# A post-norm decoder layer on one core: the end of the cross attention and the start of the experts rewritten

## The chip, the cores and the metric

The kernel runs on one core of one Trainium2 chip. Its engines work side by side and meet through semaphores: PE (TensorE, matrix products and transposes, results in PSUM), DVE (VectorE), ACT (ScalarE), POOL (GpSimd), and SP (SyncE), which here only issues DMAs. The metric is the device time of one execution in microseconds (us), as the median of several; lower is better. TensorE's clock has two levels, 1.2 and 2.4 GHz; the profile gives the granted clock as a share of the upper one.

## What is computed

One decoder layer for B = 8 batches of T = 512 tokens of D = 256 values, in float32 at the interface:

```python
x = layernorm(x + self_attention(x))            # 16 heads, decayed, levelled weights
x = layernorm(x + cross_attention(x, ctx))      # 16 heads, 1024 context tokens
x = layernorm(x + ffn(x))
# ffn, 32 experts:
probs  = softmax(x @ gate_w.T + gate_b, axis=tokens)     # per expert, over the 512 tokens
vals, idx = top_k(probs, 8)                              # each expert picks 8 tokens
merged = sum over the 8 of x[idx] * vals                 # [B, E, D]: one vector per expert
h = gelu([merged, 1] @ w1[e]);  o = [h, 1] @ w2[e]       # w1: 257x1024, w2: 1025x256
out[idx] += o * vals
```

## The kernel before, in words

There are three stages, each a block with one instruction stream per engine, and a barrier between blocks: `self_attention` (to about 620 us), `cross_attention` (to about 1717 us), `experts_and_combine` (the rest).

**Cross attention.** The work of a batch is cut into 32 steps `s`. In each step PE makes two pairs of score products (L1352, released to ACT for the exponential L1485), four products whose row maxima DVE takes (L1284, read by DVE at L1583, for the maxima 12 steps ahead), and four products of weights and values of the step before (`values`, L1306: four 32-column outputs in four column groups of the array). ACT evacuates one lane of PSUM (`cpsA`, 2 slots), DVE another (`cpsV`, 3 slots); a slot is taken in the order of a fixed job list, so PE can start a job of DVE's lane only when DVE has read the job three places before it. What closes the **previous** batch is spread over the steps of the current one, at fixed steps: MERGE (4) transposes the attention output, PROJECT_O (5) multiplies by Wo for four groups of 128 tokens, and DVE adds the residual and takes the layer norm's statistics (`stats`, `mv`); POOL makes `rstd`; NORM (7) applies it to `o2`; X2T (9) transposes `o2` for the gate; COPY_X2 (10); GATE (13) makes the gate's logits `L` and, on DVE, the 8 largest (`m8`), their negated maximum (`nm8`) and `L2`, a copy of `L` with those 8 replaced by -3e38; GATE_EXP (15): ACT takes exp of `L` and of `L2`; TOP8 (16): the difference of the two, divided by the sum, is `P8`, which is zero but for the 8 picked tokens; TOP8_T (17) transposes it; PICK (28) multiplies it with the tokens, which gives `mg` = merged; PICK_T (29) transposes `mg` into `sh.mT`. In the first batch there is no previous one; batches 1 to 7 carry this work, batches 1 to 6 in a loop on all engines but PE. After batch 7 the same steps run once more, alone: the **tail** (section `tail`, 30 steps with nothing but them).

The end of `cross_attention` on SP: in batch 7 it already loads the weights of the first two groups of experts (`w1_0`, `w2_0`, `w1_1`, `w2_1`), each group 4 experts, 4 MB of w1 and 4 MB of w2.

**Experts.** The 32 experts run in 8 groups `n`, with two buffers for w1 and two for w2. For a group PE makes the first product (L1840, 16 matmuls of 128x512, `mg4` times `w1`), transposes the result (L1850), DVE adds the bias, ACT applies gelu, PE makes the second product (L1864). SP loads ahead: `w1` of group n+2 may go when group n's first product is done (`h_full`), `w2` of group n+2 when its second product is done (`o_full`). In front of that, SP issues 14 small loads at the block's start: `b1r` (bias rows), `pick`, four times `b2` and eight times `p8`. PE at its start waits for `b1r` and transposes it (L1826), then waits for `pick` and `b2` (`c_loaded`) and for POOL's zeroed tiles (`zeroed`), and only then begins group 0. POOL at its start zeroes `hT`, `mg4[0]` and `mg4[1]` (L1775) and then copies `sh.mT` into them (L1780).

```python
            for n in range(2, GROUPS):
                sp.wait_ge(h_full, n - 1)
                load_group_weights(sp, sh, dram, 1, n % 2, n * EG)
                sp.wait_ge(o_full, n - 1)
                if n < GROUPS - 1:
                    load_group_weights(sp, sh, dram, 2, n % 2, n * EG)
```

## Time and profile before

| | |
|---|---|
| time, median of 3 runs | 1894.79 us (1892.1 to 1896.41) |
| profiled execution, its own time | 1894.31 us |
| profiled execution, span in the trace | 1892.4 us |
| busy: PE / DVE / ACT / POOL | 1698.3 / 1232.2 / 848.5 / 595.6 us |
| granted TensorE clock, mean | 0.954 |
| cross attention | about 620 to 1717 us |
| experts and combine | about 1717 to 1892 us |

The span is what the trace covers; the time is some 2 us longer. A row of a timeline gives the start, the duration, the engine, the line, the operation with output and input, how many instructions were merged into it, and in square brackets how long the engine had been idle before and what ended that. "x8" behind a float32 matmul counts passes: a float32 matmul is two of them.

### The profile page before, as it was taken

The numbers are of one execution on the slowest core, as the hardware profiler recorded it, in microseconds if no ns is written. First come the engines' busy times: TensorE is split into PE (matmuls) and PEld (weight loads), VectorE is DVE, ScalarE is ACT, GpSimd is POOL, SyncE is SP. The second block draws the span as 40 slices with busy tenths as digits, with TensorE's granted clock in tenths as the row PEclk, the third lists the DMA queues.
The fourth block names the chain that finished last, engine by engine and source line by source line (L and its number), as shares of the span: only waits on it lengthen the run. The fifth ranks groups of instructions, "written<-read, shape, count | busy, mean of one in ns | idle before, by whom it ended". The sixth has DMA issues, their size and how long they took to land. (4 is left out here: it accounts for less than half of the span.)

```text
span 1892.4 us, 48907 instructions
## 1 busy us (share of the span) xinstructions
PE 1698.3 (90%) x19908; PEld 811.1 (43%) x19908; DVE 1232.2 (65%) x2427; ACT 848.5 (45%) x1029; POOL 595.6 (31%) x955
## 2 busy tenths in 40 slices
PE   5999999999995599999999999999999999976654
PEld 3566666666664233343333333433433334232222
DVE  5767667766753577867778778678677788811004
ACT  3324334334332126655556556566555565651103
POOL 3535555555532715033043140250430410000002
PEclk8999999999997679999999999999999999988887
DMA  7000000000000321111202101111112023245994
GB/s 245 3 3 3 3 3 3 3 3 3 3 3 2 98 73 39 43 44 53 74 1 68 59 26 52 49 51 40 37 53 74 1 76 117 91 178 192 421 419 147
DMA packets 60477, 135.15 MB, mean 71 GB/s; under 512 B 11088, under 2 KB 34128, under 8 KB 52592
## 3 DMA queue, kind: packets, MB, share of 16 engines
q1 hardware_dynamic: 60272, 132.18, 19.3%
q8 instruction: 157, 2.57, 0.6%
q14 instruction: 48, 0.39, 0.1%
HBM read 89.29 MB, written 4.72 MB: 50 GB/s over the span
## 5 line engine op out<-in xcount | busy, mean ns | idle before, releaser
L1583 DVE TENSOR_REDUCE mx<-cpsV 128x1 f32<-128x512 f32 x1024 | 652.7, 685 | 196.4 <-PE cpsV L1284 182.4
L1485 ACT ACTIVATE w<-cpsA 128x1024 f32<-128x1024 f32 x512 | 496.6, 1023 | 291.1 <-PE cpsA L1352 284.5
L1284 PE MATMUL cpsV<-w 96*128 96x512 bf16 x1024 | 329.1, 393 | 34.9 <-DVE mx L1583 23.4
L1352 PE MATMUL cpsA<-w 99*128 99x512 bf16 x1024 | 273.2, 380 | 11.4 <-ACT w L1457 5.9
L1306 PE MATMUL cacc<-w 128*32 128x512 f32 x2048 | 281.1, 604 | 0.4 <-ACT w L1485 0.4
L1139 POOL TENSOR_TENSOR w<-w,zero 128x256 bf16<-128x256 f32 x84 | 48.8, 612 | 579.9 <-ACTq L1458 579.9
L1284 PEld LDWEIGHTS cpsV<-w 96*128 96x128 bf16 x1024 | 85.6, 98 | 304.9 <-DVE mx L1583 203.9
L606 ACT COPY QK<-psA 128x1024 f32<-128x1024 f32 x64 | 64.8, 1013 | 228.2 <-PE psA L363 228.2
L1352 PEld LDWEIGHTS cpsA<-w 99*128 99x128 bf16 x1024 | 92.5, 97 | 148.5 <-ACT w L1457 16.2
L714 POOL TENSOR_TENSOR VP<-V,VPF 128x128 f32<-128x128 f32 (+2 forms) x256 | 128.5, 532 | 41.4 <-PE psA L376 36.1
L363 PE MATMUL psA<-XT,wq 128*128 128x512 f32 x256 | 130.7, 634 | 4.7 <-issue 2.9
L363 PE MATMUL psA<-XT,wk 128*128 128x512 f32 x256 | 126.9, 618 | 1.3 <-DVE WT L921 1.3
L930 DVE TENSOR_TENSOR tmp<-psV,CF 128x512 f32<-128x512 f32 x64 | 44.3, 692 | 119.3 <-PE psV L426 119.0
L1914 DVE TENSOR_TENSOR z<-psE,b1T 128x256 f32<-128x256 f32 x8 | 3.4, 425 | 127.9 <-PE psE L1850 127.9
L1306 PEld LDWEIGHTS cacc<-w 128*32 128x32 f32 x2048 | 43.3, 108 | 92.8 <-issue 76.0
L937 DVE TENSOR_REDUCE Y<-tmp 128x128 f32<-128x512 f32 x64 | 67.7, 1058 | 5.1 <-issue 0.5
L1840 PE MATMUL psE<-w,mg 128*32 128x512 f32 x256 | 40.7, 794 | 29.6 <-DMA w<-in_w 26.1
L1457 ACT COPY w<-cpsA 128x1024 f32<-128x1024 f32 x24 | 24.3, 1012 | 95.7 <-PE cpsA L1254 49.7
L1271 PEld LDWEIGHTS cpsA<-w,w 128*128 128x128 f32 x512 | 58.4, 192 | 14.3 <-ACT w L1485 12.6
L1555 POOL TENSOR_TENSOR crstd<-cmv,eps 128x4 f32<-128x4 f32 x8 | 1.6, 202 | 199.4 <-DVE cmv L105 199.4
L396 PEld LDWEIGHTS psV<-QK 64*32 64x32 f32 x4096 | 41.3, 106 | 49.7 <-issue 48.4
L363 PEld LDWEIGHTS psA<-XT,wq 128*128 128x128 f32 x256 | 44.4, 193 | 41.8 <-issue 37.2
(219 smaller groups left out, 2350.1 us busy)
## 6 DMA issues: line engine op xcount, KB each, us to landing
w<-in_w SPq DMA_DIRECT2D x60, 1024.0 KB, 22.4
w<-w SPq DMA_DIRECT2D x192, 128.0 KB, 2.3
w<-w SPq DMA_DIRECT2D x192, 64.0 KB, 2.0
w<-in_ctxT SPq DMA_DIRECT2D x8, 1024.0 KB, 5.2
XT<-in_xT SPq DMA_DIRECT2D x8, 512.0 KB, 6.1
x_tok<-in_x SPq DMA_DIRECT2D x8, 512.0 KB, 10.1
w<-in_w SPq DMA_DIRECT2D x8, 512.0 KB, 21.3
out_y<-w SPq DMA_DIRECT2D x16, 256.0 KB, 2.4
```

The lines of the kernel that those rows point to most:

```text
L363: last = nc.tensor.matmul(out[:, n * T:(n + 1) * T], w[:, k, i * P:(i + 1) * P], XT[:, b, k, :], start=(k == 0), stop=(k == KD - 1))
L606: nc.scalar.copy(QK[:, i % 4, :], full(("qk", i))).then_inc(act_evac, 1)
L714: last = nc.gpsimd.tensor_tensor(VP[:, p % 2, g, 0:n, :].rearrange("q n (h c) -> q n h c", c=HD), vv.unsqueeze(1).broadcast_to([P, n, 2, HD]),
L930: nc.vector.tensor_tensor(tmp[:].rearrange("p g s (h c) -> p (g s) h c", c=HD), src.rearrange("p (h x) -> p h x", h=2)[:, :, 0:4 * HD * G] ...
L937: nc.vector.tensor_reduce(yp, tmp[:].rearrange("p g s c -> p g c s"), AX_X, ALU.add)
L1139: ops.tensor_tensor(cut(high, c), cut(r, c), zeros, ALU.add)
L1271: last = nc.tensor.matmul(out[:, c * P:(c + 1) * P], cT[:, k, c * P:(c + 1) * P], wv[:, k, hv * P:(hv + 1) * P], start=(k == 0), stop=(k = ...
L1284: nc.tensor.matmul(out, Qst[q // 2][0:ROWS, hh, g * P:(g + 1) * P], Kst[q // 2][0:ROWS, hh, half * BANK:(half + 1) * BANK], start=True, st ...
L1306: last = nc.tensor.matmul(acc[BLK * jj:BLK * (jj + 1), :], Vc[:, c, 4 * q + jj, :], Pr[:, (2 * s + jj // 2) % 4, (jj % 2) * T:(jj % 2 + 1) ...
L1352: last = nc.tensor.matmul(out[:, n * T:(n + 1) * T], Kst[q // 2][0:ROWS + 3, hh, c * P:(c + 1) * P], Qst[q // 2][0:ROWS + 3, hh, :], start ...
L1485: nc.scalar.activation(Pr[:, (2 * s + pp) % 4, :], src, ACT.Exp, scale=CA_SCALE).then_inc(act_evac, 1)
L1583: nc.vector.tensor_reduce(mx[:, q % 2, row, k % 2:k % 2 + 1], full(m[k]), AX_X, ALU.max).then_inc(dve_evac, 1)
```

## The change

Six edits. **(a)** PICK: the four products of the token groups, which were added up in one 32-row output, go to four 32-row outputs in four column groups of the array; `mg` now holds four partial sums one above the other, and PICK_T adds them up while transposing, by a product with `sum4` (four identity matrices of 32 in a column) in place of two transposes. `mg` is evacuated on 128 partitions, split by `k`. **(b)** One exponential: ACT takes exp of `L` alone, into `EL`, as soon as `nm8` is there (DVE's `match_replace` goes on meanwhile), and TOP8 keeps those elements of `EL` whose `L2` is below -1e38. **(c)** NORM counts `x2_ready` up once per token group, with no drain, and X2T waits group by group. **(d)** In PROJECT_O the statistics of groups 0 and 1 are taken between the additions of groups 1 and 2. **(e)** Experts, PE: group 0's first product goes to the front; the transposes of `b1r` and the wait for `pick` and `b2` follow it; the wait for `zeroed` is ACT's alone. **(f)** Experts, POOL: `mg4[0]` is zeroed and filled first, then `mg4[1]`, then `hT` is zeroed. DVE makes `sum4` once at the start of the cross attention.

```diff
@@ PE, cross attention
                         if s == PICK:
                             out = take_v("mg", after="p8T")
                             for g in range(G):
-                                last = nc.tensor.matmul(out[0:E, 0:D], P8T[:, g, :], o2[:, g, :],
-                                                        start=(g == 0), stop=(g == G - 1))
+                                last = nc.tensor.matmul(out[E * g:E * (g + 1), 0:D], P8T[:, g, :], o2[:, g, :],
+                                                        start=True, stop=True)
...
                             for k in range(KD):
-                                last = nc.tensor.transpose(out[:, k * P:(k + 1) * P],
-                                                           mgp[:].rearrange("e (p k) -> e k p", k=KD)[:, k, :], sh.ident[:])
+                                last = nc.tensor.matmul(out[:, k * P:k * P + E], mgp[:, k, :], sum4[:],
+                                                        start=True, stop=True)
...
                     if prev and s == X2T:
-                        pe.wait_ge(x2_ready, b)
-                        transpose_x("x2T", o2)
+                        out = take_a("x2T")
+                        for g in range(G):
+                            pe.wait_ge(x2_ready, (b - 1) * G + g + 1)
+                            for k in range(KD):
+                                last = nc.tensor.transpose(out[:, k * T + g * P:k * T + (g + 1) * P],
+                                                           o2[:, g, k * P:(k + 1) * P], sh.ident[:])
+                        last.then_inc(act_full, 1)
@@ ACT, cross attention
                         if s == GATE_EXP:
                             act.wait_ge(l_ready, b)
-                            nc.scalar.activation(L[:], L[:], ACT.Exp, bias=nm8[:, 0:1], accum_out=sume[:, 0:1])
-                            nc.scalar.activation(L2[:], L2[:], ACT.Exp, bias=nm8[:, 0:1])
+                            nc.scalar.activation(EL[:], L[:], ACT.Exp, bias=nm8[:, 0:1], accum_out=sume[:, 0:1])
                             act.drain().then_inc(e_ready, 1)
@@ DVE, cross attention
+            nc.vector.tensor_reduce(sum4[:], sh.ident[:].rearrange("p (g e) -> p e g", e=E), AX_X, ALU.add)
...
                             for g in range(G):
                                 nc.vector.tensor_tensor(o2[:, g, :], full(("wo", g))[:, 0:D], xb(b - 1)[:, g, :], ALU.add
                                                         ).then_inc(dve_evac, 1)
+                                if g % 2:
+                                    dve.drain()
+                                    for gg in (g - 1, g):
+                                        nc.vector.bn_stats(stats[:, gg, :], o2[:, gg, :])
                             dve.drain()
-                            layer_norm_stats(nc, dve, o2, stats, mv).then_inc(var, 1)
+                            for g in range(G):
+                                last = nc.vector.bn_aggr(mv[:, g, :], stats[:, g, :])
+                            last.then_inc(var, 1)
...
                                 nc.vector.tensor_scalar(o2[:, g, :], o2[:, g, :], mv[:, g, 0:1], rstd[:, g, 0:1],
-                                                        ALU.subtract, ALU.mult)
-                            dve.drain().then_inc(x2_ready, 1)
+                                                        ALU.subtract, ALU.mult).then_inc(x2_ready, 1)
...
-                            nc.vector.tensor_scalar(nm8[:], m8[:, 0:1], -1.0, None, ALU.mult)
+                            nc.vector.tensor_scalar(nm8[:], m8[:, 0:1], -1.0, None, ALU.mult).then_inc(l_ready, 1)
                             nc.vector.match_replace(L2[:], m8[:], L[:], -3.0e38)
-                            dve.drain().then_inc(l_ready, 1)
+                            dve.drain()
...
-                            nc.vector.tensor_tensor(P8, L[:], L2[:], ALU.subtract)
+                            nc.vector.scalar_tensor_tensor(out=P8, in0=L2[:], scalar=-1.0e38, in1=EL[:],
+                                                           op0=ALU.is_lt, op1=ALU.mult)
...
-                            nc.vector.tensor_copy(mg, full("mg")[0:E, 0:D]).then_inc(dve_evac, 1)
+                            nc.vector.tensor_copy(mgp[:], full("mg")[:, 0:D].rearrange("q (p k) -> q k p", k=KD)
+                                                  ).then_inc(dve_evac, 1)
@@ PE, experts
-            pe.wait_ge(b_loaded, 16)
-            for c in range(FC):
-                last = nc.tensor.transpose(psB[:, c * E:(c + 1) * E],
-                                           b1r[:].rearrange("e (p c) -> e c p", c=FC)[:, c, :], sh.ident[0:E, 0:E])
-            last.then_inc(b1_full, 1)
-            pe.wait_ge(c_loaded, 16 * (1 + BT))
-            pe.wait_ge(zeroed, 1)
             for n in range(GROUPS):
...
                 last.then_inc(h_full, 1)
-                if n:
+                if n == 0:
+                    pe.wait_ge(b_loaded, 16)
+                    for c in range(FC):
+                        last = nc.tensor.transpose(psB[:, c * E:(c + 1) * E],
+                                                   b1r[:].rearrange("e (p c) -> e c p", c=FC)[:, c, :], sh.ident[0:E, 0:E])
+                    last.then_inc(b1_full, 1)
+                    pe.wait_ge(c_loaded, 16 * (1 + BT))
+                else:
                     pick_rows(n - 1)
```

**PE at the start of the experts.** The stream of PE from the last step of the tail on; `psE` is the PSUM of the experts, `mg_0` is `mg4[0]`, `w_0` a weight buffer, `sum` is `sum4`. Before:

```order
L1388 MATMUL cpsV<-o,P8T 32x256 x4
L1394 MATMUL cpsV<-ident,mg 128x128 x2
L1068 UNCONDITIONAL_BRANCH
L1793 UNCONDITIONAL_BRANCH
L1826 MATMUL psE<-ident,b1r 128x32 x8
L1840 MATMUL psE<-w_0,mg_0 32x512 x16
L1850 MATMUL psE<-ident,hS 128x128 x8
```

And in the changed kernel:

```order
L1388 MATMUL cpsV<-o,P8T 32x256 x4
L1394 MATMUL cpsV<-sum,mg 128x32 x2
L1068 UNCONDITIONAL_BRANCH
L1807 UNCONDITIONAL_BRANCH
L1847 MATMUL psE<-w_0,mg_0 32x512 x16
L1854 MATMUL psE<-ident,b1r 128x32 x8
L1864 MATMUL psE<-ident,hS 128x128 x8
```

The first product (16 matmuls) has moved ahead of the 8 transposes of `b1r`; the two transposes of `mg` have become two products of 32 columns.

**POOL at the start of the experts.** The memsets and the copies that release PE's first product, of before and of the change:

```order
-L1775 MEMSET hT 128x1024
-L1775 MEMSET mg_0 128x256
-L1775 MEMSET mg_1 128x256
-L1780 COPY mg_0<-mT 128x8x8
-L1780 COPY mg_1<-mT 128x8x8
```

```order
+L1788 MEMSET mg_0 128x256
+L1794 COPY mg_0<-mT 128x8x8
+L1788 MEMSET mg_1 128x256
+L1794 COPY mg_1<-mT 128x8x8
+L1791 MEMSET hT 128x1024
```

One memset and one copy stand before `mg_0` is ready, where there were three memsets and one copy.

**DVE at PROJECT_O and after, in the tail.** Additions of the residual (`o<-cpsV,x_tok`), statistics (`BN_STATS`), their aggregate, the norm and the gate. Before:

```order
L1640 TENSOR_TENSOR o<-cpsV,x_tok 128x256 x4
L102 BN_STATS cstats<-o 128x6 x4
L105 BN_AGGR cmv<-cstats 128x2 x4
L1647 TENSOR_SCALAR o<-o,cmv,crstd 128x256 x4
L1651 TENSOR_SCALAR L<-cpsV,gb 32x512
```

And in the changed kernel:

```order
L1645 TENSOR_TENSOR o<-cpsV,x_tok 128x256 x2
L1650 BN_STATS cstats<-o 128x6 x2
L1645 TENSOR_TENSOR o<-cpsV,x_tok 128x256 x2
L1650 BN_STATS cstats<-o 128x6 x2
L1653 BN_AGGR cmv<-cstats 128x2 x4
L1658 TENSOR_SCALAR o<-o,cmv,crstd 128x256 x4
L1661 TENSOR_SCALAR L<-cpsV,gb 32x512
```

Two of the four statistics have moved between the additions; nothing else changes its place on this engine, in the tail or in the batches.

## Rows read from the trace of the kernel before

**Rows 1.** Busy time by stretch: PE, PEld, DVE, ACT, POOL, then clock, DMA share, GB/s

```profile
760.00:1500.00 740.00, 709.90 (x3890) 276.95 (x3883) 561.01 (x1136) 422.38 (x457) 199.27 (x320) 1.00 0.14 46
1683.00:1717.00 34.00, 18.39 (x52) 10.26 (x50) 10.15 (x32) 4.39 (x6) 1.31 (x3) 0.70 0.54 225
1755.00:1805.00 50.00, 28.75 (x300) 12.86 (x296) 0.85 (x2) 3.97 (x7) 0.47 (x2) 0.85 1.01 420
```

**Rows 2.** Timeline at the start of the experts

```profile
1716.90 0.96 POOL L1775 MEMSET hT<- 128x1024 f32 x1 [20.15 <-POOLq L1068]
...
1718.53 0.41 POOL L1780 COPY mg<-mT 128x64 f32<-128x64 f32 x2 [0.17 <-issue]
...
1719.15 1.09 PE L1826 MATMUL psE<-ident,b1r 32*128 32x32 f32 x8 [2.85 <-DMA b1r<-in_w]
...
1722.38 0.89 SPq L1754 DMA_DIRECT2D p<-p_scratch  x2
...
1723.81 6.04 PE L1840 MATMUL psE<-w,mg 128*32 128x512 f32 x32 [3.57 <-DMA b<-in_w]
...
1729.92 2.00 SPq L998 DMA_DIRECT2D w<-in_w  x4
```

**Rows 3.** Timeline, the first products of groups 3 and 7

```profile
1763.60 4.93 PE L1840 MATMUL psE<-w,mg 128*32 128x512 f32 x32 [6.07 <-DMA w<-in_w]
...
1843.14 6.11 PE L1840 MATMUL psE<-w,mg 128*32 128x512 f32 x32 [6.21 <-DMA w<-in_w]
```

**Rows 4.** Timeline of the tail: last addition, statistics, norm, transposes

```profile
1692.95 0.42 DVE L1640 TENSOR_TENSOR o<-cpsV,x_tok 128x256 f32<-128x256 f32 x1 [0.44 <-PE cpsV L1368]
1693.47 1.40 DVE L102 BATCH_NORM_STATS2 cstats<-o 128x6 f32<-128x256 f32 x4
...
1696.78 1.38 DVE L1647 TENSOR_SCALAR o<-o,cmv,crstd 128x256 f32<-128x256 f32 x4 [1.46 <-POOL crstd L1557]
...
1698.25 1.97 PE L1246 MATMUL cpsA<-ident,o 128*128 128x128 f32 x8 [5.34 <-DVEq L1649]
```

**Rows 5.** Timeline of the tail: replacing the eight, exponentials, reciprocal

```profile
1706.74 0.66 DVE L1657 MATCH_REPLACE8 L<-m,L 32x512 f32<-32x512 f32 x1
1707.46 0.72 ACT L1499 ACTIVATE L<-L,nm 32x512 f32<-32x512 f32 x1 [5.25 <-DVEq L1658]
...
1708.18 0.70 ACT L1500 ACTIVATE L<-L,nm 32x512 f32<-32x512 f32 x1
1708.94 0.15 DVE L1663 RECIPROCAL rsum<-sume 32x1 f32<-32x1 f32 x1 [1.54 <-ACTq L1501]
```

**Rows 6.** Timeline of the tail: pick, its copy, its transposes

```profile
1711.79 3.50 PE L1388 MATMUL cpsV<-o,P8T 128*32 128x256 f32 x8 [0.38 <-DVE P8T L1668]
...
1715.33 0.41 DVE L1671 COPY mg<-cpsV 32x256 f32<-32x256 f32 x1 [3.60 <-PE cpsV L1388]
1715.80 0.51 PE L1394 MATMUL cpsV<-ident,mg 128*128 128x128 f32 x2 [0.51 <-DVE mg L1671]
```

**Rows 7.** Timeline inside a batch, around its PICK step

```profile
1174.20 1.06 PE L1306 MATMUL cacc<-w 128*32 128x512 f32 x8
...
1177.03 1.70 PE L1388 MATMUL cpsV<-o,P8T 128*32 128x256 f32 x7
...
1177.96 1.29 DVE L1583 TENSOR_REDUCE mx<-cpsV 128x1 f32<-128x512 f32 x2
...
1179.17 0.40 DVE L1671 COPY mg<-cpsV 32x256 f32<-32x256 f32 x1
...
1180.17 1.29 DVE L1583 TENSOR_REDUCE mx<-cpsV 128x1 f32<-128x512 f32 x2 [0.59 <-PE cpsV L1284]
```

**Rows 8.** Timeline inside a batch, PE after its PROJECT_O step

```profile
1094.32 0.39 PE L1284 MATMUL cpsV<-w 96*128 96x512 bf16 x1 [0.54 <-DVE mx L1583]
```

**Rows 9.** Timeline of batch 7, ACT after the PICK step

```profile
1674.54 1.94 ACT L1485 ACTIVATE w<-cpsA 128x1024 f32<-128x1024 f32 x2 [1.74 <-PE cpsA L1352]
```

**Rows 10.** Timeline, nearest passes with full weights and few columns

```profile
763.66 3.84 PE L1271 MATMUL cpsA<-w,w 128*128 128x128 f32 x32
```

More of the change, by code:

```diff
@@ L1097, in cross_attention @@
         stats, mv, rstd = sb("cstats", [P, G, 6]), sb("cmv", [P, G, 2]), sb("crstd", [P, G, 1])
-        L, L2 = sb("L", [E, T]), sb("L2", [E, T])
-        P8p, mgp = sb("P8", [P, T]), sb("mg", [P, D])
-        P8, mg = P8p[0:E], mgp[0:E]
+        L, L2, EL = sb("L", [E, T]), sb("L2", [E, T]), sb("EL", [E, T])
+        P8p, mgp = sb("P8", [P, T]), sb("mg", [P, KD, P])
+        P8, sum4 = P8p[0:E], sb("sum4", [P, E])
         m8, nm8, sume, rsum = sb("m8", [E, 8]), sb("nm8", [E, 1]), sb("sume", [E, 1]), sb("rsum", [E, 1])
@@ L1494, in body @@
                         if s == COPY_X2:
-                            act.wait_ge(x2_ready, b)
+                            act.wait_ge(x2_ready, b * G)
                             nc.scalar.copy(xb(b - 1), o2[:]).then_inc(x2_copied, 1)
@@ L1521, in _ @@
         def _(pool):
-            for t in (Vc, NM, P8p, mgp):
+            for t in (Vc, NM, P8p):
                 nc.gpsimd.memset(t[:], 0.0)
@@ L1773, in _ @@
         def _(pool):
-            for t in (hT, mg4[0], mg4[1]):
-                last = nc.gpsimd.memset(t[:], 0.0)
-            pool.drain().then_inc(zeroed, 1)
             for n in range(GROUPS):
+                if n < 2:
+                    nc.gpsimd.memset(mg4[n][:], 0.0)
+                    pool.drain()
+                if n == 2:
+                    nc.gpsimd.memset(hT[:], 0.0).then_inc(zeroed, 1)
                 if n >= 2:
```

## The prediction

> **What bounds the kernel now.** I read the busy time by stretch first. In the batches of the cross attention PE is busy 709.9 of 740 us with the clock at its upper level, so PE sets the pace there and DVE, at 561, has little slack. In the tail (1683 to 1717) PE is busy 18.4 of 34 us at a granted clock of 0.70 and every other engine less: nothing is full, a chain of dependent steps is the bound. From 1755 on the DMA engines are at 1.01 with 420 GB/s: the stream of expert weights is the bound [rows 1]. That stream of 48 MB (six groups of w1 and w2) cannot start before group 0's first product is done: the timeline has the product at 1723.81, 6.04 us long, and the first weight load right behind it at 1729.92 [rows 2]. So what makes the first product end earlier starts the stream earlier, and with it all that follows. Three places then count for the sum: the seven closings inside the batches, the tail, and the start of the experts.
>
> **Start of the experts (e, f).** Before, PE stood idle for `b1r`, transposed it (1.09 us), then waited for `b2` until 1723.81. Now it needs only `mg4[0]` and weights that were loaded long before. POOL begins at 1716.90; zeroing 1024 columns took 0.96 us, so 256 take at most 0.3; one copy is half of 0.41 [rows 2]. With 0.15 us for a drain and hand-over that makes 1717.55 for the start of the product, 6.26 earlier than 1723.81. If the product keeps its 6.04 us, it ends at 1723.6. What is late next is SP: its 14 small loads end at 1722.38 + 0.89 = 1723.27 [rows 2], so the load could not go before 1723.3 anyway. Gain 6.25. The product's duration depends on the clock: later ones took 4.93 and 6.11 us [rows 3], and wholly at 1.2 GHz it would be about 7.0 (8 passes of `values` take 1.06 at the upper level, some 0.2 of it the pipeline's end [rows 7]; 32 passes are 3.4, doubled 6.8, plus 0.2). So the gain lies between 5.3 (7.0 us product) and 6.6 (SP's queue). The moved transposes of `b1r` (1.09) now lie beside ACT's evacuation of the product and cost at most 0.1; memset of `hT` is done before ACT needs it. The cover for these is the weight stream, which has 4 MB under way by then; without it they would cost their 1.1 us.
>
> **Tail.** Each term is on the chain, so it counts in full. (d) Two of four statistics (half of 1.40) fall into PE's time for groups 2 and 3, where DVE idled 0.44 before the addition [rows 4]: -0.70. (c) The transposes started at 1698.25, behind all four normalizations; the first group is ready after a quarter of 1.38, at 1697.13, and two transposes (0.49) take longer than one normalization (0.35), so PE runs through from 1697.2: -1.04 [rows 4]. (b) ACT can start when `match_replace` starts (1706.74), 0.66 earlier, and the second exponential's 0.70 goes, of which I leave 0.1 for the read of the first one's accumulator, which it hides now. So the reciprocal comes at 1707.7 in place of 1708.94: -1.26. `match_replace` ends at 1707.40, just in time [rows 5]. The comparison and product that replaces the subtraction has the same two inputs and size and is taken as equal. (a) The pick took 3.50 us, 8 passes one behind the other at the lower clock level [rows 6]. In four column groups they run side by side: `values` has that form, four outputs of 32 rows, 8 passes of twice the columns, in 1.06 at the upper level [rows 7], so about 0.43 for the passes there, 0.86 at the lower level, 1.1 with the end: -2.4. The copy `mg` reads as many elements per partition: 0.41. PICK_T has four passes in place of two, with full weights and few columns. Two took 0.51 [rows 6]; four cost 1.02 at that pace, or 0.5 by the pace of 3.84 us for 32 [rows 10], which is the upper level: +0.45, bounds 0 and +0.5. Sum of the tail: -0.70 - 1.04 - 1.26 - 2.4 + 0.45 = -4.95.
>
> The Trainium skill, in "TensorE: Matmul & The Clock Gate", section "LDWEIGHTS (loading the stationary operand)", speaks against (a) here: a weight load takes time by its columns, about 107 ns for 128, so shrinking the moving side to 32 columns saves little. By it four loads would be 0.43 us and the term near 0; the row at the lower level asks for more.
>
> **Inside the batches.** (a) Around the PICK step in a batch the passes take 1.7 us one after the other (eight times 0.21) and would take 0.43: PE is freed 1.28. But DVE is next. After the pick it still has two maxima, 1177.96 to 1179.25, then the copy of `mg` to 1179.57, and only at 1180.17 the next maximum, after an idle 0.59 [rows 7]. With PE earlier DVE goes on at 1179.6, and PE waits for its slots: so 0.6 of the 1.28 arrives. In batch 7, which has no maxima at step 28, ACT stood idle 1.74 before it [rows 9] and PE's 1.28 arrives nearly whole: 1.15. (d) After PROJECT_O, PE waits 0.54 for DVE, which is behind by its 1.4 us of statistics [rows 8]; the same row is there in batches 1 to 6, 0.53 to 0.54. With 0.7 us of statistics moved into DVE's idle gaps of 0.44 between additions, that wait goes and PE's next issues move up: 0.6, bounds 0.5 and 0.7. (b) The exponential dropped lies on ACT, which has room; DVE is full at the TOP8 step, so nothing arrives. (c) needs nothing here: X2T is two steps behind NORM. PICK_T's two more passes cost PE two times 0.12 [rows 10], half of it behind other waits: +0.1. Per batch 0.6 + 0.6 - 0.1 = 1.1, times six is 6.6; batch 7 gives 1.15 + 0.6 - 0.1 = 1.65. Together -8.2. Bounds: 0, if all of it is swallowed by DVE; 7 x (1.28 + 0.7) = 13.9, if all arrives. `sum4` and one memset fewer lie at the block's start under PE's first products: 0.
>
> **Sum.** -8.2 - 4.95 - 6.25 = -19.4. Against the profiled execution's own 1894.31 that is 1874.9; the median of the runs is 0.5 higher, so 1875.
>
> **Rivals.**
> *DVE swallows the batches' part.* The closing work in the batches then brings 0 and only tail and start count: -11.2, 1883. For it: DVE has waits of its own to give and the maxima follow back to back at these places. Against it: the idle 0.59 and PE's wait of 0.54 are in the trace and must close. Chance 0.15. The Trainium skill, in "TensorEngine Tiling (Array Packing)", section "PSUM Bottleneck", says this: tiling speeds up the array but not the reading of PSUM, which may become the bound after it. The trace agrees for half of the gain.
> *PE's time counts in full.* PE is at 96% in the batches, and after a few steps DVE could have caught up: -13.9 - 4.95 - 6.25 = -25.1, 1869.5. Against it: the slots of `cpsV`. Chance 0.12.
> *The early product starts nothing.* If SP or the stream itself is later than I think (the small loads and w1 share the DMA engines; or the end hangs on PE's last group rather than on the stream), the 6.25 is lost: -13.15, 1881.5. Against it: in rows 1 the DMA engines are full. Chance 0.07.
> *No change.* The stages hide it all, within 3.8 us. I see no cover for the tail's chain: 0.03.
> *Slower.* PE's clock falls inside the batches. Every us of PE work at 1.2 GHz costs another us. Place: the steps where column groups now run side by side and leave PE short gaps waiting for DVE. 2.8 us of such work in each of seven batches eats the 19.4, and from there it is slower; 5 us per batch would cost 35 and give 1894.8 - 19.4 + 35 = 1910. Against it: the granted clock is 1.00 over 740 us although PE waits 0.5 to 1 us at several places per batch [rows 1, 8]. Chance 0.03.
>
> **How the numbers follow.** The likeliest case, 0.60, is 1875, own range 1872 to 1878 (batches 5.5 to 11, start 5.3 to 6.6). The range 1869 to 1883.5 reaches to the cases on both sides. Changes within 0.2% (3.8 us) can't be told from none here. Faster 0.94, same 0.03, slower 0.03.
>
> **What would show it.** First product at about 1.0 us after the block's start, before `b1r`'s transposes, and the first w1 load at its end, some 6.7 us after the block's start in place of 13.0; the stretch from there to the end unchanged at 162.5. In the tail the pick near 1.1 us, its transposing near 1.0, the reciprocal 0.95 after `match_replace` begins. In the batches a period shorter by 1.1 us, DVE's idle 0.59 gone and PE's 0.54 gone. Wrong it would be most easily in the batches: if the period moves by 0 or by 2, the interplay of DVE and PE was misread; and if the product takes 7 us, the start is worth a microsecond less.

## The result, and the profile after

| | before | after |
|---|---|---|
| time, median | 1895.15 us (1892.1 to 1896.41, 4 runs) | 1879.16 us (1874.29 to 1881.4, 4 runs) |
| profiled execution: its time, span | 1894.31, 1892.4 us | 1881.4, 1879.5 us |
| granted TensorE clock, mean | 0.954 | 0.949 |

The ratio is 0.9912, interval 0.9895 to 0.9929: 16.7 us less, where the sum had 19.4. The forecast's 1875 lies 4.2 us below the new median and the range holds it. One execution of all, 2007.93 us at a mean clock of 0.821 (in "More work for PE instead"), was in a slow state of the chip and is left out. Two numbers ask for a closer look: the profiled execution gained only 12.9 us of span (it was the slowest of its four), and the mean clock went down. So the three places of the sum are read one by one. The stretches between the same marks in both traces:

| stretch, us | before | after | difference | forecast |
|---|---|---|---|---|
| block's start to first exponential of the batches | 684.35 | 684.58 | +0.2 | 0 |
| first to last exponential of the batches | 995.28 | 993.86 | -1.4 | -8.2 |
| last exponential to the end of `mT` (tail) | 36.98 | 32.33 | -4.65 | -4.95 |
| end of `mT` to the first w1 load | 13.31 | 6.71 | -6.6 | -6.25 |
| first w1 load to the end | 162.46 | 162.06 | -0.4 | 0 |

Tail and start came as computed; in the batches 6.8 us are missing. The busy time by stretch of the changed kernel, columns as in [rows 1]:

```profile
760.00:1500.00 740.00, 710.50 (x3903) 277.37 (x3902) 563.28 (x1136) 419.68 (x450) 198.00 (x318) 0.99 0.14 46
1683.00:1717.00 34.00, 21.49 (x86) 11.19 (x86) 9.39 (x27) 3.78 (x5) 3.13 (x7) 0.60 0.59 234
...
1755.00:1805.00 50.00, 31.70 (x344) 14.55 (x336) 1.27 (x3) 5.26 (x9) 0.71 (x3) 0.86 1.01 421
```

The first row answers to [rows 1]: PE is busy about as long, but the clock there reads 0.99 in place of 1.00. That hundredth of 740 us is the riddle of this case.

**Start of the experts**, the timeline that answers to [rows 2]:

```profile
1711.04 0.32 POOL L1788 MEMSET mg<- 128x256 f32 x1 [16.12 <-POOLq L1068]
...
1711.49 0.24 POOL L1794 COPY mg<-mT 128x64 f32<-128x64 f32 x1
...
1711.87 5.05 PE L1847 MATMUL psE<-w,mg 128*32 128x512 f32 x32 [1.42 <-POOL mg L1794]
...
1716.54 0.89 SPq L1766 DMA_DIRECT2D p<-p_scratch  x2
...
1716.85 1.06 PE L1854 MATMUL psE<-ident,b1r 32*128 32x32 f32 x8
...
1717.47 2.10 SPq L998 DMA_DIRECT2D w<-in_w  x4
```

The product begins 0.83 us after POOL does and is done at 1716.92; the load goes only at 1717.47, behind SP's last small load (1716.54 + 0.89 = 1717.43). The bound of 6.6 that the prediction gave for a faster product is what came: SP's queue is late next.

**Tail**, the rows that answer to [rows 4 to 6]:

```profile
1691.77 0.42 DVE L1645 TENSOR_TENSOR o<-cpsV,x_tok 128x256 f32<-128x256 f32 x1 [0.56 <-PE cpsV L1368]
1692.29 0.75 DVE L1650 BATCH_NORM_STATS2 cstats<-o 128x6 f32<-128x256 f32 x2
...
1694.96 1.39 DVE L1658 TENSOR_SCALAR o<-o,cmv,crstd 128x256 f32<-128x256 f32 x4 [1.47 <-POOL crstd L1561]
...
1695.52 1.94 PE L1415 MATMUL cpsA<-ident,o 128*128 128x128 f32 x8 [3.78 <-DVE o L1658]
...
1704.01 0.66 DVE L1667 MATCH_REPLACE8 L<-m,L 32x512 f32<-32x512 f32 x1
1704.05 0.72 ACT L1504 ACTIVATE EL<-L,nm 32x512 f32<-32x512 f32 x1 [4.60 <-DVE nm L1666]
...
1704.91 0.15 DVE L1673 RECIPROCAL rsum<-sume 32x1 f32<-32x1 f32 x1 [0.24 <-ACTq L1505]
...
1707.76 1.08 PE L1388 MATMUL cpsV<-o,P8T 128*32 128x256 f32 x8 [0.38 <-DVE P8T L1679]
...
1708.91 0.42 DVE L1682 COPY mg<-cpsV 128x256 f32<-128x256 f32 x1 [1.20 <-PE cpsV L1388]
...
1709.39 1.06 PE L1394 MATMUL cpsV<-sum,mg 128*128 128x32 f32 x4 [0.55 <-DVE mg L1682]
```

Statistics behind the last addition: 1.40 to 0.75. Start of the normalization to start of the transposes: 1.47 to 0.56. Start of `match_replace` to the reciprocal: 2.20 to 0.90. Pick: 3.50 to 1.08. Its transposing: 0.51 to 1.06.

One thing in this stretch was luck. The product with Wo at its start is the same in all kernels, but its time hangs on the granted clock. In the traces of before, of the change, and of a second execution of the change (experiment "The changed kernel once more"):

```profile
1687.32 5.59 PE L1368 MATMUL cpsV<-cwo,oT 128*128 128x256 f32 x16 [1.10 <-ACT oT L1447]
```

```profile
1685.26 6.47 PE L1368 MATMUL cpsV<-cwo,oT 128*128 128x256 f32 x16 [1.10 <-ACT oT L1452]
```

```profile
1684.67 3.72 PE L1368 MATMUL cpsV<-cwo,oT 128*128 128x256 f32 x16 [1.10 <-ACT oT L1452]
```

With the transposes in front of it, which took 1.95, 1.09 and 1.09, it comes to 7.54, 7.56 and 4.81. The first two happen to be equal, so the difference of the two stretches shows the edits alone. In the second execution of the change the stretch took 29.57 in place of 32.33, and these products account for all of the 2.8.

**Inside a batch.** Answers to [rows 8] (the first row) and [rows 7] (the rest):

```profile
1094.40 0.65 PE L1284 MATMUL cpsV<-w 96*128 96x512 bf16 x2
...
1178.97 0.64 PE L1388 MATMUL cpsV<-o,P8T 128*32 128x256 f32 x8
...
1179.91 1.29 DVE L1588 TENSOR_REDUCE mx<-cpsV 128x1 f32<-128x512 f32 x2
1181.11 0.42 DVE L1682 COPY mg<-cpsV 128x256 f32<-128x256 f32 x1
1181.44 1.28 DVE L1588 TENSOR_REDUCE mx<-cpsV 128x1 f32<-128x512 f32 x2
```

PE's wait of 0.54 is gone, the pick's passes take 0.64 in place of 1.7, and the idle 0.59 of DVE behind the copy is gone too. These signs of the forecast all came. To see why the gain didn't arrive, take the time of every step: the distance between every second exponential of ACT. For batch 2, all steps that differ by 0.1 us or more, worked out from the exponentials' starts:

```
step                6     15     16     17     28     29
before           3.54   3.47   2.29   5.54   4.60   3.40
after            2.89   2.86   2.81   5.69   4.15   3.30
difference      -0.65  -0.61  +0.52  +0.15  -0.45  -0.10
```

The sum is -1.14, and -1.1 was forecast. Batch 6 gained 1.35 and batch 7 2.0. If all had gone so, the batches would have gained some 9 us. But in batches 1, 3, 4 and 5 step 17 took 7.08 to 7.27, and step 5 of batch 0, where no closing exists, was longer as well. The timeline at step 17 of batch 3, changed kernel (PE, then DVE):

```profile
1138.21 0.38 PE L1284 MATMUL cpsV<-w 96*128 96x512 bf16 x1
1139.74 0.39 PE L1284 MATMUL cpsV<-w 96*128 96x512 bf16 x1 [1.15 <-DVE mx L1588]
1140.34 0.66 PE L1325 MATMUL cpsV<-ident,OT 128*128 128x128 f32 x4 [0.21 <-DVE mx L1588]
1141.03 0.83 PE L1382 MATMUL cpsV<-ident,P 128*128 128x128 f32 x4
1141.79 1.94 PE L1306 MATMUL cacc<-w 128*32 128x512 f32 x8
1143.66 1.03 PE L1284 MATMUL cpsV<-w 96*128 96x512 bf16 x2
...
1137.07 1.15 DVE L1674 SCALAR_TENSOR_TENSOR P<-L,EL 32x512 f32<-32x512 f32 x1
1138.30 0.79 DVE L1677 TENSOR_SCALAR P<-P,rsum 32x512 f32<-32x512 f32 x1
```

and the same place before the change:

```profile
1139.39 0.39 PE L1284 MATMUL cpsV<-w 96*128 96x512 bf16 x1 [1.01 <-DVE mx L1583]
...
1140.67 0.63 PE L1382 MATMUL cpsV<-ident,P 128*128 128x128 f32 x4
1141.23 1.06 PE L1306 MATMUL cacc<-w 128*32 128x512 f32 x8
```

The same eight passes of `values` take 1.94 in place of 1.06. Busy time by stretch, 3 us of it and then the whole time at the lower level, changed kernel:

```profile
1141.00:1144.00 3.00, 2.97 (x13) 0.79 (x14) 1.55 (x7) 0.00 (x0) 0.00 (x0) 0.55 0.43 135
1141.30:1144.70 3.40, 3.40 (x15) 0.80 (x14) 1.65 (x8) 0.00 (x0) 0.00 (x0) 0.50 0.38 118
```

The granted clock is 0.50 for 3.4 us: PE ran at 1.2 GHz there, busy without a pause, soon after the wait of 1.15 (0.7 to 1.6 us after it ended, in the four batches). Each such fall cost 1.4 to 1.6 us. The profile of before has none in the batches, that of after has five: some 7.5 us, which covers the 6.8 that are missing.

Batch 6 had no fall, and it had no long wait either. There POOL, which is a pass ahead and in batches 1 to 5 adds `bo` to a later batch's tokens beside DVE's two operations (first row, batch 3), stands idle; both operations are shorter (the rest, batch 6):

```profile
1136.95 3.41 POOL L1538 TENSOR_TENSOR x_tok<-x_tok,bo 128x256 f32 x4 [0.17 <-issue]
```

```profile
1527.12 0.66 DVE L1674 SCALAR_TENSOR_TENSOR P<-L,EL 32x512 f32<-32x512 f32 x1
...
1527.86 0.47 DVE L1677 TENSOR_SCALAR P<-P,rsum 32x512 f32<-32x512 f32 x1
...
1528.99 0.39 PE L1284 MATMUL cpsV<-w 96*128 96x512 bf16 x1 [0.35 <-DVE mx L1588]
```

So PE waits 0.35 for DVE in batch 6 (and in batch 7) in place of 1.15, and step 17 takes 4.88 in place of 5.69.

### The profile page after: what moved, and what is told of

It is laid out like the page before. It is cut to its first block and busy times, and to the rows that moved or that the text cites. A ratio compares the mean times of both kernels' runs of the same rounds, so it can differ in the third digit from the quotient of the medians.

```text
span 1879.5 us, 48932 instructions
## 1 busy us (share of the span) xinstructions
PE 1693.5 (90%) x19924; PEld 810.0 (43%) x19924; DVE 1234.0 (66%) x2428; ACT 844.4 (45%) x1021; POOL 595.4 (32%) x954
## 3 DMA queue, kind: packets, MB, share of 16 engines
q1 hardware_dynamic: 60272, 132.18, 19.4%
## 5 line engine op out<-in xcount | busy, mean ns | idle before, releaser
L1588 DVE TENSOR_REDUCE mx<-cpsV 128x1 f32<-128x512 f32 x1024 | 652.6, 685 | 201.3 <-PE cpsV L1284 189.1
L1271 PE MATMUL cpsA<-w,w 128*128 128x128 f32 x512 | 61.4, 278 | 0.9 <-ACT w L1462 0.9
```

The source lines that it names most:

```text
L1271: last = nc.tensor.matmul(out[:, c * P:(c + 1) * P], cT[:, k, c * P:(c + 1) * P], wv[:, k, hv * P:(hv + 1) * P], start=(k == 0), stop=(k = ...
L1588: nc.vector.tensor_reduce(mx[:, q % 2, row, k % 2:k % 2 + 1], full(m[k]), AX_X, ALU.max).then_inc(dve_evac, 1)
```

## The experiments

Theory **C** in the expectations: the clock falls at step 17 because PE waits longer for DVE at TOP8. Its rival **P**: the falls are chance and have nothing to do with the change. All ratios are against runs of the kernel before on the same chip (median 1895.3 to 1895.6), and the differences in us are worked out from the ratios; those of the medians differ from them by up to 1.7 us. Each profile shows one execution.

**The start alone (edits e and f).** Before, with the order of the changed kernel in the experts:

```diff
+                if n < 2:
+                    nc.gpsimd.memset(mg4[n][:], 0.0)
+                    pool.drain()
...
+                if n == 0:
+                    pe.wait_ge(b_loaded, 16)
```

> The kernel before with parts (e) and (f) alone: first product first, mg4[0] zeroed first. Both theories below say the same here: the first w1 load goes some 6.6 us earlier after the block's start (13.0 before), since SP's 14 small loads end then; the stream and everything behind it follow, -6.2 to -6.6 us in time (about 0.9967). If instead the end hung on something else than the stream, the time would stay within 2 us of before although the load goes earlier.

Measured 1889.27 us, ratio 0.9966 (0.9954 to 0.9978): -6.4. End of `mT` to the first load is 6.69. The start's term stands.

**Two exponentials again (edit b undone).** The changed kernel with this turned back:

```diff
-                            nc.scalar.activation(EL[:], L[:], ACT.Exp, bias=nm8[:, 0:1], accum_out=sume[:, 0:1])
+                            nc.scalar.activation(L[:], L[:], ACT.Exp, bias=nm8[:, 0:1], accum_out=sume[:, 0:1])
+                            nc.scalar.activation(L2[:], L2[:], ACT.Exp, bias=nm8[:, 0:1])
```

> The changed kernel with part (b) undone: two exponentials, the subtraction, l_ready after the replacement. Theory C (the clock): with one exponential ACT lets PE reach the TOP8 step 0.6 us earlier, PE then waits that much longer for DVE, and the granted clock falls there in some batches (four of seven in the profile), 1.4 us each. Undone, the falls at step 17 go (0 or 1 left) and each batch keeps its gain: the tail loses 1.26 us, the batches win 3 to 6, so 1 to 4 us faster than the changed kernel, about 1876. Rival P (chance): the falls hit any kernel by the clock's own timing, whatever the wait; then 3 to 5 falls remain and the time is 1.3 us above the changed kernel.

Measured 1877.15 us, ratio 0.9909 (0.9895 to 0.9922). PE's wait at TOP8 is back at 1.01, no fall of the clock in the batches, and the same 3 us of batch 3 read

```profile
1141.00:1144.00 3.00, 3.00 (x21) 0.99 (x24) 2.53 (x9) 0.87 (x1) 0.00 (x0) 1.00 0.36 112
```

First to last exponential: 985.88, which is 9.4 less than before. So (a), (c) and (d) alone give the batches' whole term.

**The pick alone (edit a).** Before, with the pick in four column groups and its transposing by `sum4`:

```diff
-                                last = nc.tensor.matmul(out[0:E, 0:D], P8T[:, g, :], o2[:, g, :],
-                                                        start=(g == 0), stop=(g == G - 1))
+                                last = nc.tensor.matmul(out[E * g:E * (g + 1), 0:D], P8T[:, g, :], o2[:, g, :],
+                                                        start=True, stop=True)
```

> The kernel before with part (a) alone. By the prediction: -2.4 + 0.5 in the tail and -0.45 in each of batches 1 to 6, -1.15 in batch 7: -5.8 us without falls of the clock. Theory C: no falls, since nothing at step 16 and 17 changes: 1889.3. Rival P: one to five falls of 1.4 us, in any step, 1891 to 1896.

Measured 1888.04 us, ratio 0.9966 (0.9954 to 0.9979): -6.5. Two falls, though the wait at TOP8 is that of before: one at step 5 of batch 0, one at step 17 of batch 3. Theory C wanted none. So a fall at that place doesn't need the longer wait.

**The changed kernel once more.**

> The changed kernel once more, for the number of falls in a second profile on the chip that the others ran on. Theory C: again two to six falls, nearly all at step 17. Rival P: a number between 0 and 5 at steps that differ from those of the first profile. The time 1874 to 1882.

Measured 1877.82 us (1876.08 to 1880.17), ratio 0.9908 (0.9895 to 0.9922). Its profile has three falls, at step 17 of batches 3, 4 and 5; the batches take 990.54. The same instructions, 3.3 us apart from the first profile in this stretch: how many falls an execution gets is open each time.

**More work for DVE at TOP8.** Before, with the subtraction made twice:

```diff
                             dve.drain()
+                            nc.vector.tensor_tensor(P8, L[:], L2[:], ALU.subtract)
+                            dve.drain()
```

> The kernel before with DVE's subtraction at TOP8 made twice, a pure addition of 0.66 to 1.1 us of DVE's work between two maxima (0.7 in the tail). PE waits for DVE there, so its wait grows by as much. Theory C (the clock falls where PE waits long enough around step 16): the profile shows falls of the clock at step 17, which before had none, and the time grows by 7 times 1.1 plus 0.7 plus 1.4 per fall, 10 to 17 us. Rival P: no falls at step 17 beyond chance (at most one), 8 us.

Measured 1908.12 us, ratio 1.0069 (1.0052 to 1.0085): +13. PE's wait in batch 3 is now

```profile
1147.50 0.39 PE L1284 MATMUL cpsV<-w 96*128 96x512 bf16 x1 [2.16 <-DVE mx L1583]
```

Step 17 takes 6.68 in place of 5.54 in batch 3, and in batches 6 and 7, where the extra subtraction is shorter, 0.75 more; that makes 7.2 for the seven batches. Step 17 of batches 1, 2, 4 and 5 (not 3) takes 8.07 to 8.27, a fall of the clock in each, 6.1 together. In batches 6 and 7 PE's wait is 1.02 and 1.10, and no fall came.

**The statistics alone (edit d).** Before, with this in PROJECT_O:

```diff
+                                if g % 2:
+                                    dve.drain()
+                                    for gg in (g - 1, g):
+                                        nc.vector.bn_stats(stats[:, gg, :], o2[:, gg, :])
```

> The kernel before with part (d) alone. By the prediction -0.6 in each of seven batches at the step after PROJECT_O and -0.7 in the tail: -4.9 us, 1890.4. Nothing at step 16 changes, so theory C expects no falls there. If PE caught up elsewhere anyway, only the tail's -0.7 would be seen.

Measured 1889.81 us (1886.9 to 1896.26), ratio 0.9979 (0.9968 to 0.9989): -4.0 (-5.6 by the medians). No fall in the batches of its profile, and they take 4.5 less, where 4.2 was expected. But of its ten executions two took 1893.57 and 1896.26 at a mean clock of 0.949 and 0.948, where the others have 0.950 to 0.954. They have no trace, so where their clock was low isn't known; that falls are rare in this kernel is shown for one execution only.

**One exponential alone (edit b).** Before, with `EL` and the comparison:

```diff
-                            nc.vector.tensor_tensor(P8, L[:], L2[:], ALU.subtract)
+                            nc.vector.scalar_tensor_tensor(out=P8, in0=L2[:], scalar=-1.0e38, in1=EL[:],
+                                                           op0=ALU.is_lt, op1=ALU.mult)
```

> The kernel before with part (b) alone. Theory C: the tail gains 1.26 us, the batches 0.1 each, and falls of the clock appear at step 17 (three to five, 1.4 us each, none in the profile of before): the net is +1 to +5 us, slower than before. Rival P: no or one fall, net -2 us.

Measured 1892.12 us, ratio 0.9985 (0.9976 to 0.9994): -2.9. PE's wait is 1.16, as in the changed kernel, but only one fall came (step 17 of batch 1), where C wanted three to five. The first to the last exponential takes 997.09, 1.8 more than before: with the fall's 1.7 taken out that is no change, so the edit brings nothing in the batches. In the tail its row is worth 1.3; the rest of the 2.9 has no row of its own. (The tail of its profile is 4.6 shorter than that of before, but 2.7 of that is the product with Wo and the transposes before it, 4.81 in place of 7.54, at the upper clock.)

**The multiplication by 1/sum given to ACT.** The changed kernel, with DVE's last operation of TOP8 moved:

```diff
+                        if s == TOP8:
+                            act.wait_ge(p8_raw, b)
+                            nc.scalar.activation(P8, P8, ACT.Identity, bias=zero[0:E, 0:1], scale=rsum[:, 0:1]
+                                                 ).then_inc(p8_ready, 1)
...
-                            nc.vector.tensor_scalar(P8, P8, rsum[:, 0:1], None, ALU.mult).then_inc(p8_ready, 1)
+                            dve.drain().then_inc(p8_raw, 1)
```

> The changed kernel with the multiplication by 1/sum at TOP8 moved from DVE to ACT (an activation with a per-partition scale). DVE has 0.79 us less at the step where PE waits 1.15 for it. Theory C: no falls at step 17, and the 0.5 us that step 17 gave back is kept: -0.7 per batch and -1.4 for each of the three to five falls; the tail loses 0.3: 7 to 10 us below the changed kernel, about 1869. Rival P: the falls stay, -4.5 us, 1873.

Measured 1873.93 us (1873.31 to 1874.66), ratio 0.9888 (0.9871 to 0.9904): the fastest kernel here, and the one with the least spread. Timeline of batch 3:

```profile
1137.04 0.81 ACT L1509 ACTIVATE P<-P,zero,rsum 32x512 f32<-32x512 f32 x1 [1.10 <-DVEq L1681]
...
1137.92 0.39 PE L1285 MATMUL cpsV<-w 96*128 96x512 bf16 x1 [0.58 <-DVE mx L1593]
```

The wait fell from 1.15 to 0.58, steps 16 and 17 take 7.9 together in place of 8.5, no fall in the batches, and they take 982.75. That is 3 to 3.6 less than in the two profiles of the changed kernel with their falls taken out (986.3 and 985.8), where theory C had 4.9. The time is at rival P's 1873, though the falls are gone, and not at C's 1869. One reason can be read from the stretches behind the batches: they take 201.3 us here and 198.2 in the second profile of the changed kernel, the first product alone 6.42 in place of 4.93.

**The same, with the eight `p8` loads behind group 2's w1 load.**

```diff
                 load_group_weights(sp, sh, dram, 1, n % 2, n * EG)
+                if n == 2:
+                    for j in range(BT):
...
+                            sp.dma_start(p8[rows, h, :], sh.p8_dram[:, t0:t0 + T]).then_inc(p_loaded, 16)
```

> As the one before, and SP issues the eight p8 loads behind the first w1 load of the experts in place of ahead of it, since the profile of the changed kernel has SP still issuing (to 1717.43) when the first product ended (about 1716.96). Gain 0.5 us where the product takes 5 us and 0 where it takes 6 or more; the stream has eight small loads more in it, 0.5 MB or 1.2 us if they take their share of the DMA engines instead of fitting beside it. So between -0.5 and +1.2 against the kernel before it in this list.

Measured 1876.15 us, ratio 0.9894 (0.9877 to 0.991): no gain, and 2.2 more than the kernel above by the medians. Busy time by stretch, of this kernel and then of the one above (the last column is GB/s):

```profile
1716.00:1726.00 10.00, 8.77 (x120) 4.37 (x116) 0.42 (x1) 1.79 (x3) 0.24 (x1) 1.00 1.02 361
```

```profile
1716.00:1726.00 10.00, 8.77 (x124) 4.45 (x120) 0.43 (x1) 1.61 (x3) 0.24 (x1) 1.00 1.01 422
```

In the middle of the weight stream the small loads take the DMA engines' time at 361 in place of 422 GB/s, and group 3's product starts 43.90 us after the first one in place of 40.24: 3.7 later, where the expectation had at most 1.2 for their bytes. The first product took 6.56 in this profile and 6.42 in that of the kernel above, so there was nothing to gain from an earlier SP, as the expectation had it for a product of 6 us or more.

**More work for PE instead.** The changed kernel, with the third maximum's product of TOP8 made three times, so that PE computes while DVE works. The extra products change no value:

```diff
+                        for _ in range(again if k == 2 else 0):
+                            nc.tensor.matmul(out, Qst[q // 2][0:ROWS, hh, g * P:(g + 1) * P],
```

> The changed kernel, and at TOP8 (step 16) PE makes the third maximum's product three times in place of once, into the same slot: 0.43 us more work for PE in a wait of 1.15 us, ending as DVE comes for it, so nothing is later (at most 0.1 us per batch). Theory C: what brings the clock down is PE's lack of work at this place; with the gap partly filled the falls at step 17 become fewer (0 or 1 against 4 and 3 in two profiles of the changed kernel), and the time drops by 1.4 us for each. If the falls come from the wait itself or from DVE's lateness whatever PE does, 3 to 5 stay and the time is that of the changed kernel.

Measured 1875.64 us as the median of four executions (1874.24 to 1877.46; 1876.04 with the slow one), ratio 0.9898 (0.9882 to 0.9913). Timeline of batch 3:

```profile
1138.03 0.39 PE L1288 MATMUL cpsV<-w 96*128 96x512 bf16 x1 [0.73 <-DVE mx L1592]
```

The gap is 0.73, with DVE's work and its end as before, and no fall at step 17: steps 16 and 17 take 3.24 + 5.27 = 8.51, as long as 2.81 + 5.69 = 8.50 in the changed kernel where no fall came. One fall came at step 5 of batch 0. At these two steps the extra work for PE cost nothing. Batches 1 to 7 take 869.3 together, against 868.4 and 867.7 in the two profiles of the changed kernel with their falls taken out; that is 0.1 to 0.2 us per batch, at other steps.

**Counting the falls.** Over all twelve profiles, step 17 of batches 1 to 5, where POOL works beside DVE:

| PE's wait for DVE at TOP8 | kernels | falls | of batches |
|---|---|---|---|
| 0.58 to 0.75 | scale on ACT (two), filler | 0 | 15 |
| 1.01 to 1.04 | before, start, two exponentials, pick, statistics | 1 | 25 |
| 1.14 or more | changed (two), one exponential, subtraction twice | 12 | 20 |

In batches 6 and 7 no fall came at this step in any profile; the wait was 0.35 or less, but for 1.02 and 1.10 with the subtraction made twice.

This joins both theories. P is right that a single execution can't be foretold: with the wait at 1.14 or more the four profiles had 4, 3, 1 and 4 falls, and step 5 of batch 0, with the same code and a wait of 1.42 to 1.44 us in every kernel, fell in 5 of 12 profiles. C is right that the change matters: 12 of 20 against 1 of 25 is hardly chance, even with the profiles taken as four and five single cases (4, 3, 1, 4 against 0, 0, 0, 1, 0). But the batches of one profile follow each other at nearly equal distances (127 to 133 us), so if the clock's own timing plays a part, they aren't independent tries; no experiment moved a batch in time and left its waits alone. That it is PE's gap and not DVE's work that counts is suggested by the filler, which leaves DVE alone, but not shown: it is one profile of five batches, and with (b) alone one profile with the full gap had one fall in five.

## Why the prediction was right, point by point

**Start.** Forecast -6.25, measured -6.6 between the marks and -6.4 in time when alone. The product took 5.05 in place of the 6.04 assumed, so that SP's queue became the limit, at the bound named for it. That it did so here hung on the clock: with the same start, the product took 6.00 with two exponentials and 6.42 with the scale on ACT, and the first load went 7.18 and 7.59 us after `mT`, not 6.71.

**Tail.** Forecast -4.95, measured -4.65. By terms (forecast, measured): statistics -0.70, -0.65; transposes -1.04, -0.91; reciprocal -1.26, -1.30; pick -2.4, -2.42; its transposing +0.45, +0.55. The terms add up to -4.73. The terms are right, each on its own row. That the whole stretch agrees as well is luck, as the same clock hit the Wo product in both profiles: in the second profile of the change the stretch is 7.4 shorter than before. The Trainium skill's "TensorE: Matmul & The Clock Gate", section "LDWEIGHTS (loading the stationary operand)", would have made the transposing term near 0; the row at the lower clock level (1.06 for four passes) decides against it here. At the upper level four passes take 0.63 in batches 1 to 6 and 0.53 in batch 7.

**Inside the batches.** Forecast -8.2. Without the falls the two profiles of the change give -9.0 and -9.5, and the kernel with two exponentials, which had no fall, -9.4.
- The statistics: -0.6 forecast, -0.65 at step 6. Right.
- The pick: 0.6 of 1.28 should arrive, less 0.1 for its transposing; steps 28 and 29 gave -0.45 and -0.10. In batch 7, -1.27 at step 28 and +0.14 at step 29, forecast -1.15 and +0.1. Right, and so was the reason, DVE as the next in line. The page "TensorEngine Tiling (Array Packing)", section "PSUM Bottleneck", of the Trainium skill agrees with it for more than half of the freed time.
- One exponential: "nothing arrives" was right in the sum and wrong in the way. 0.61 arrives at step 15, since DVE begins TOP8 earlier, and 0.67 is given back at steps 16 and 17. PE's wait for DVE there grows from 1.01 to 1.15.
- The clock. This is the one step that failed. Under "Slower" the falling clock was set aside with "the granted clock is 1.00 over 740 us although PE waits 0.5 to 1 us at several places". The trace of before is one execution. It showed five waits of 1.01 to 1.03 and one of 1.42 (batch 0, step 5) without a fall; but at that last place, with the same instructions, the clock fell in 5 of the 12 profiles, so its absence in one trace was no proof. And one of the edits made the wait at TOP8 longer. The place was wrong too: it was not the steps with column groups but the one beside DVE's TOP8. In the first profile of the change the falls took back 7.5 of 9.0 us, in the second 4.7 of 9.5. How many came in the executions without a trace isn't known; the medians of the changed kernel (1879.16 and 1877.82) lie 4.2 and 2.8 above 1875, which two or three falls would fill. The range holds the time all the same, since the rest of the batches' term came in full and a little more.

**Rivals.** "DVE swallows the batches' part" would have needed steps 6 and 28 to stay; they moved. "PE's time counts in full" would have needed -1.28 at step 28. "Slower" had the right cause, a fall of the clock, at the wrong step and it asked for 2.8 us in each of seven batches, where the two profiles lost 7.5 and 4.7 us in all. "The early product starts nothing" is excluded by the first experiment. Together (e, f), (a) and (d) alone gave 6.4 + 6.5 + 4.0 = 16.9, and (b) alone 2.9; the whole gave 16.7 to 17.4, some 2.4 to 3.1 less than the four together. Taking (b) back changes the time by nothing measurable (1877.15 against 1877.82). Its row in the tail is worth 1.3 us, and it brings nothing before that. Edit (c) alone was not tried; its 0.91 is read from the tail's rows.

## What to carry to other kernels

Compare two traces step by step, by a mark that comes once per step, before a small gain over many batches is judged: a fall of the clock of 3.4 us is lost in a mean of 0.99, and stands out at once in the step's time. Take a second profile of the same kernel before something that one trace doesn't show is called absent. Ahead of an edit, look for the longest wait of the bound engine and ask whether the edit makes it longer: work moved off the engine that is waited for (here one multiplication, DVE to ACT: 3 to 4 us, by 982.75 in the batches against 985.8 and 986.3 for the changed kernel without its falls, and by the medians 1873.93 and 1877.82, whose ratios' intervals overlap) is worth more than work taken off an engine that has room. Look at a third engine too: batch 6, where POOL is idle beside DVE, shows step 17 0.8 us shorter with no edit at all. Moving POOL's addition of `bo` out of TOP8 was not tried. And when small loads stand in front of a stream, measure both orders: in the stream they can cost more than ahead of it.

## What the runs showed of the hardware

- The granted clock fell to the lower level for 3.4 us in the middle of dense PE work: at step 17 in 12 of 20 batches where PE had stood 1.14 us or more, in one of 25 where it had stood 1.01 to 1.04, in none of 15 where it had stood 0.58 to 0.75. What else decides in a single batch stays open.
- DVE's comparison and product over 32x512 took 1.14 to 1.18 us in batches 1 to 5, where POOL works beside it, and 0.66 in batches 6 and 7 and in the tail, where POOL is idle, in all profiles; the subtraction took 1.06 to 1.13 and 0.66 to 0.68, the multiplication by 1/sum 0.79 and 0.47. DVE's and PE's work in batch 6 is that of batches 1 to 5, so POOL's is the likely reason; no run moved it.
- The self-attention stage, with the same code in all kernels, took 683.8 to 687.5 us up to the first exponential. A part of the spread of the times comes from there, and no small edit of the later stages can be read from two spans without taking it out.
- In the tail the same product with Wo took 3.72 to 6.47 us by the granted clock of its stretch.
